# A two-expert network in a fused decoder: plain scatters into one row per choice, tables of slots with the tile innermost

## What is computed

```
x = x + L0_attn(layernorm(x)); x = x + L0_xattn(layernorm(x), ctx, mask)
x = x + L0_ffn(layernorm(x))       # below
x = x + L1_attn(layernorm(x)); x = x + L1_xattn(layernorm(x), ctx); x = x + L1_ffn(layernorm(x))

def L0_ffn(x):                     # 8 experts, 2 per token, 256 rows per expert
    top_vals, top_ids = top_k(x_flat @ router_w.T + router_b, 2)
    top_probs = softmax(top_vals)
    for e in range(8):
        tok, slot = nonzero(top_ids == e, size=256, fill_value=(N, 0))
        xin = x_pad[tok]; a = xin @ W[e]; b = xin @ V[e]
        out = out.at[tok].add((a * silu(b)) @ W_out[e] * probs_pad[tok, slot])
```

## Time and profile before

| | us |
|---|---|
| median of 3 runs (lowest, highest) | 2030.23 (2028.16, 2034.81) |
| the profiled execution | 2028.86 |
| its span in the trace | 2026.4 |
| slots stage c0, first to last vector instruction | 711.8 to 767.1 |
| two-expert stage, first gather to last vector instruction | 768.6 to 846.8 |
| wide attention, from its first ACT row | 848.6 |
| slots stage c1, first to last vector instruction | 1763.5 to 1807.7 |

### The profile page before, as it was taken

The page is one execution under the profiler, slowest core; times in us unless marked ns, Lnnn a source line. Parts: engine busy times, 40 slices in busy tenths (PEclk is TensorE's granted clock), DMA queues, the critical chain, the costliest instruction groups (busy, mean ns, idle before and its releaser), DMA issues. The chain is left out here.

```text
span 2026.4 us, 71865 instructions
## 1 busy us (share of the span) xinstructions
PE 1673.6 (83%) x28813; PEld 1383.6 (68%) x28815; DVE 1468.7 (72%) x3171; ACT 963.1 (48%) x1975; POOL 1379.7 (68%) x1173
## 2 busy tenths in 40 slices
PE   4899997899997806299899999999999659637776
PEld 3677775677776805178788888888888549536665
DVE  6888886688886691389788888888888565764443
ACT  3677775677774371033343444434343261234444
POOL 3677775677775335278788888888888427638887
PEclk9899998899998957599999999999999879869999
DMA  8100000000000322400000000000000054422221
GB/s 224 49 1 0 0 0 6 17 17 16 16 14 5 103 83 32 93 3 3 0 0 0 0 0 0 0 0 0 0 0 0 17 179 138 121 66 68 66 66 50
DMA packets 98085, 73.70 MB, mean 36 GB/s; under 512 B 11790, under 2 KB 87504, under 8 KB 97600
## 3 DMA queue, kind: packets, MB, share of 16 engines
q1 hardware_dynamic: 86176, 55.74, 9.5%
q0 software_dynamic: 8496, 15.61, 3.1%
q10 hardware_dynamic: 3312, 0.97, 0.2%
HBM read 49.19 MB, written 23.56 MB: 36 GB/s over the span
## 5 line engine op out<-in xcount | busy, mean ns | idle before, releaser
L1257 POOL TENSOR_TENSOR wa_rot<-wa_rot,wa_cross 128x1024 f32<-128x1024 f32 x128 | 302.7, 2365 | 99.6 <-DVE wa_cross L1440 99.6
L1437 DVE TENSOR_TENSOR wa_rot<-wa_ps_qk,cos 128x1024 f32<-128x1024 f32 x128 | 155.8, 1217 | 61.5 <-PE wa_ps_qk L1310 61.1
L1409 ACT COPY wa_pt<-wa_ps_svt 128x1024 f32<-128x1024 f32 x64 | 64.9, 1015 | 270.2 <-PE wa_ps_svt L1346 270.2
L333 POOL TENSOR_TENSOR sa_sd<-sa_sd,sa_mx 128x1024 f32<-128x1024 f32 x64 | 121.7, 1902 | 90.1 <-DVE sa_mx L545 90.1
L1263 POOL TENSOR_TENSOR wa_sd<-wa_sd,wa_mx 128x1024 f32<-128x1024 f32 x64 | 121.7, 1902 | 71.7 <-DVE wa_mx L1453 71.7
L333 POOL TENSOR_TENSOR ca_sd<-ca_sd,ca_mx 128x1024 f32<-128x1024 f32 x64 | 121.7, 1902 | 69.1 <-DVE ca_mx L545 69.1
L1310 PE MATMUL wa_ps_qk<-wa_xt,l_wq 128*128 128x128 f32 x1024 | 132.9, 284 | 5.8 <-issue 4.4
L1310 PE MATMUL wa_ps_qk<-wa_xt,l_wk 128*128 128x128 f32 x1024 | 134.3, 286 | 2.9 <-DVE wa_cross L1440 2.9
L1370 PE MATMUL wa_ps_o<-l_wo,wa_ot 128*128 128x128 f32 x1024 | 128.6, 280 | 8.8 <-ACT wa_ot L1415 8.8
L1310 PEld LDWEIGHTS wa_ps_qk<-wa_xt,l_wq 128*128 128x128 f32 x1024 | 120.8, 194 | 13.6 <-issue 10.7
L1370 PEld LDWEIGHTS wa_ps_o<-l_wo,wa_ot 128*128 128x128 f32 x1024 | 122.7, 196 | 9.4 <-ACT wa_ot L1415 9.4
(11 more groups left out here) (338 smaller groups left out, 4767.9 us busy)
## 6 DMA issues: line engine op xcount, KB each, us to landing
x_res<-in_x_dram SPq DMA_DIRECT2D x16, 256.0 KB, 6.7
ca_ctx_t<-in_ctx_t_dram SPq DMA_DIRECT2D x64, 64.0 KB, 1.8
x_dram<-x_res SPq DMA_DIRECT2D x16, 256.0 KB, 2.3
xn_dram<-c_xn SPq DMA_DIRECT2D x16, 256.0 KB, 2.7
x_res<-x_dram SPq DMA_DIRECT2D x16, 256.0 KB, 5.4
cs_ctx_t<-in_ctx_t_dram SPq DMA_DIRECT2D x16, 256.0 KB, 2.9
l_ffn<-in_f_w_dram SPq DMA_DIRECT2D x2, 2048.0 KB, 11.3
cm_ctx<-in_ctx_dram SPq DMA_DIRECT2D x16, 256.0 KB, 3.1
```

The lines of the kernel that those rows point to most:

```text
L333: pool.tensor_tensor(sd[:, v % 4], sd[:, v % 4], mx[:, v % 4].unsqueeze(2).to_broadcast([P, H0, SEQ]), ALU.subtract).then_inc(sub_ready, 1)
L1257: pool.tensor_tensor(rot[n][:, v % 2], rot[n][:, v % 2], cross[n][:], ALU.add)\
L1437: dve.tensor_tensor(rot[n][:, v % 2].rearrange("p f j t -> p (f j) t"), src.rearrange("p f j t -> p (f j) t"), bc(k.cos[:], 1, 2 * QUADS), ...
```

## The change

- The zeros and the store of x in xp go. A new DRAM tensor choice_dram has a row for each (choice, token). Self-attention's SP list fills it with zeros, 16 transfers of 512 KB, behind its loads; POOL clears their source first.
- The slots stage no longer lists weights (2 lists for both calls). The number of a row is choice x 8192 + token. row_hot is stored with the tile innermost [row, tile], compared in bf16 with a loaded constant `index` (2 MB, in c1 also `tile_number` of 1.2 MB; SP issues them ahead of the stores of rows). In c0 the vector engine makes all of it. Tiles go in two halves, and TensorE takes a half when it is listed; its weights are now columns 64 elements apart. In c1 the ring of normalised rows is 2 groups deep in place of 4.
- The two-expert stage scatters unweighted rows without an add and without waiting for the scatter before; ACT copies them out of PSUM. x is not loaded back: SP loads the choices' rows of 4 groups (two transfers each), and the vector engine multiplies and adds those of group 0 and takes its statistics.
- Wide attention does that for groups 1 to 15: ACT multiplies by the token's weight (`weigh`, 8 instructions), POOL adds the two choices (`pair_up`), the vector engine adds them to x (`combine`) and takes statistics. `combined_in` says in which step ACT and POOL do it. ACT waits for statistics at the start of steps 4 and 16.

```diff
+        zero_rows = None if cross else sb("zero_rows", [P, ZEROED, P])
...
+                sp.wait_ge(zeroed, 1)
+                for n in range(2 * NT // ZEROED):
+                    rows = k.choice_dram[n * ZEROED:(n + 1) * ZEROED].rearrange("n p c -> (n p) c")
+                    sp.dma_start(rows.rearrange("(q r) c -> q r c", q=P), zero_rows[:]).then_inc(zeros_stored, 16)
...
-            sp.dma_start(k.x_dram[NT:NT + NE * CAP // P].rearrange("n p c -> p n c"),
-                         bc(zero_row[:], 1, NE * CAP // P)).then_inc(zeros_stored, 16)
-            for g in range(NG):
-                sp.wait_ge(x_added, g + 1)
-                sp.dma_start(k.x_dram[rows(g)].rearrange("n p c -> p n c"), k.x_res[:, rows(g)]).then_inc(x_stored, 16)
...
+        part = sb("part", [P, 2, top, NT], BF16)
...
+        index = sb("index", [P, P, NT], BF16)
+        tile_number = sb("tile_number", [P, NT, NS], BF16) if top == 1 else None
+        row_hot = [sb(f"row_hot{n}", [P, P, NT], BF16) for n in range(top)]
...
+        by_dve = NT if top == 2 else NT * 5 // 8
+        distance = None if top == 2 else sb("distance", [P, P, NT - by_dve], BF16)
+        HALVES = [slice(0, NT // 2), slice(NT // 2, NT)]
...
+        RING = 4 if top == 2 else 2
...
+            sp.dma_start(index[:].rearrange("p a t -> p (a t)"), k.in_index.to_broadcast([P, P * NT]))\
+                .then_inc(index_loaded, 16)
...
+                for t in range(by_dve, NT):
+                    op = act.activation(distance[:, :, t - by_dve], k.iota_s[:], ACT.Square, bias=neg_part[:, t:t + 1])
+                op.then_inc(distance_ready, 1)
+                act.wait_ge(distance_ready, 1)
+                act.activation(row_hot[top - 1][:, :, by_dve:NT], distance[:], ACT.Relu, scale=-1.0, bias=one[:])\
...
+                for half in range(2):
+                    pe.wait_ge(listed_ready, 2 * n + half + 1)
+                    if HALVES[half].stop > by_dve:
+                        pe.wait_ge(hot_ready, 1)
+                    for t in range(HALVES[half].start, HALVES[half].stop):
+                        mm = pe.matmul(ps_l[:, 0:lists * NS], row_hot[n][:, :, t],
+                                       listed[n][:, t].rearrange("p l s -> p (l s)"),
+                                       start=(n == 0 and t == 0), stop=(n == top - 1 and t == NT - 1))
+            mm.then_inc(listed_made, 1)
...
+            dve.wait_ge(index_loaded, 16 if top == 2 else 32)
+            for n in range(top):
+                for half, of in enumerate(HALVES):
+                    mine = slice(of.start, min(of.stop, by_dve))
+                    op(dve.tensor_tensor(row_hot[n][:, :, mine], index[:, :, mine], bc(part[:, 1, n, mine], 1, P), ALU.is_equal))
+                    shape = [P, NT // 2, NS]
+                    op(dve.tensor_tensor(tile_hot[:, of], bc(k.iota_s[:, 0:NS], 1, NT // 2),
+                                         part[:, 0, n, of].unsqueeze(2).to_broadcast(shape), ALU.is_equal))
+                    number = (k.iota_s1[:, n * NT + of.start:n * NT + of.stop].unsqueeze(2).to_broadcast(shape) if top == 2 else
+                              tile_number[:, of])
+                    op(dve.tensor_tensor(listed[n][:, of, 0], tile_hot[:, of], number, ALU.mult))
+                    op(dve.tensor_scalar(listed[n][:, of, 1], tile_hot[:, of], k.place[:], None, ALU.mult))
+                    dve.memset(zeros[:, 0:1], 0.0).then_inc(listed_ready, 1)
...
-                op(dve.tensor_tensor(w[:, 3], w[:, 1], w[:, 2], ALU.mult))
-                op(dve.tensor_copy(parts[:, :, 0], w[:, 2:4]))
-                for n in range(3):
-                    op(dve.tensor_copy(parts_bf[:, :, n], parts[:, :, n]))
-                    if n < 2:
-                        op(dve.tensor_tensor(parts[:, :, n + 1], parts[:, :, n], parts_bf[:, :, n], ALU.subtract))
...
-                    op(dve.tensor_tensor(row_hot[n][:, 0:mine], bc(k.iota_s[:], 1, mine),
-                                         part[:, 1, n, 0:mine].unsqueeze(2).to_broadcast([P, mine, P]), ALU.is_equal))
-                op(dve.tensor_tensor(tile_hot[:], bc(k.iota_s[:, 0:NS], 1, NT),
-                                     part[:, 0, n].unsqueeze(2).to_broadcast([P, NT, NS]), ALU.is_equal))
-                op(dve.tensor_tensor(listed[n][:, :, 0], tile_hot[:], k.iota_s1[:, 0:NT].unsqueeze(2).to_broadcast([P, NT, NS]),
-                                     ALU.mult))
-                op(dve.tensor_scalar(listed[n][:, :, 1], tile_hot[:], k.place[:], None, ALU.mult))
-                for q in range(2, lists):
-                    op(dve.tensor_tensor(listed[n][:, :, q], tile_hot[:],
-                                         parts_bf[:, n, q - 2].unsqueeze(2).to_broadcast([P, NT, NS]), ALU.mult))
-                dve.memset(zeros[:, 0:1], 0.0).then_inc(listed_ready, 1)
-            dve.wait_ge(listed_made, top)
...
+                op(dve.tensor_scalar(w[:, 2], w[:, 1], 1.0, None, ALU.add))
+                op(dve.reciprocal(k.w_token[:, 0], w[:, 2]))
+                op(dve.tensor_tensor(k.w_token[:, 1], w[:, 1], k.w_token[:, 0], ALU.mult))
+            dve.wait_ge(listed_made, 1)
...
+            op(dve.scalar_tensor_tensor(out=id_i[:], in0=table[:, 0], scalar=float(P), in1=table[:, 1],
+                                        op0=ALU.mult, op1=ALU.add))
+            op(dve.tensor_scalar(k.gather_idx[:, 0:NS].bitcast(I32), id_i[:], NT * P - 1, None, ALU.bitwise_and))
+            op(dve.scalar_tensor_tensor(out=ids[:, 3], in0=table[:, 0], scalar=0.0, in1=k.empty_id[:, 0:NS],
+                                        op0=ALU.is_equal, op1=ALU.mult))
+            op(dve.tensor_tensor(k.scatter_idx[:, 0:NS], id_i[:], ids[:, 3], ALU.add))
...
+            def scatter(e):
+                pool.wait_ge(y_ready, e + 1)
+                for n in range(HALVES * e, HALVES * (e + 1)):
+                    pool.indirect_dma_start(choice_rows, bass.IndirectOffsetOnAxis(ap=k.scatter_idx[:, n:n + 1], axis=0),
+                                            y[:, n], None, bounds_check=2 * NT * P - 1, oob_is_err=False).then_inc(added[e], 16)
...
-                if e:
-                    pool.wait_ge(added[e - 1], 16 * HALVES)
-                for half in range(HALVES):
-                    n = HALVES * e + half
-                    pool.indirect_dma_start(k.x_rows, bass.IndirectOffsetOnAxis(ap=k.scatter_idx[:, n:n + 1], axis=0),
-                                            y[:, n], None, compute_op=ALU.add).then_inc(added[e], 16)
...
+                    act.copy(y[:, HALVES * e:HALVES * (e + 1)].rearrange("p n c -> p (n c)"), ps_y[:, 0:CAP])\
+                       .then_inc(y_ready, 1)
...
-            for n in range(NT // GROUP):
-                sp.dma_start(k.x_res[:, n * GROUP:(n + 1) * GROUP],
-                             k.x_dram[n * GROUP:(n + 1) * GROUP].rearrange("n p c -> p n c"))\
-                    .then_inc(k.x_loaded[n], 16)
+            for g in range(k.choice_bufs):
+                load_choices(sp, k, g)
...
-                    dve.tensor_scalar(y[:, n], ps_y[:, half * P:(half + 1) * P], k.w_slot[:, n:n + 1], None,
-                                      ALU.mult).then_inc(y_ready, 1)
...
+            def add_choices(g):
+                dve.wait_ge(k.choice_loaded[g], 32)
+                for n in range(2):
+                    if n:
+                        dve.wait_ge(added_up, 1)
+                    for m in range(GROUP):
+                        t = g * GROUP + m
+                        op = dve.scalar_tensor_tensor(out=k.x_res[:, t], in0=k.choice[:, g, n, m],
+                                                      scalar=k.w_token[:, n, t:t + 1], in1=k.x_res[:, t],
+                                                      op0=ALU.mult, op1=ALU.add)
+                    op.then_inc(added_up, 1)
+                dve.wait_ge(added_up, 2)
+            first = LoadedStats(dve, k, st, (st_ready, mv_ready, newton), 0, 1, add_choices)
...
+def load_choices(sp, k, g):
+    for n in range(2):
+        tiles = slice(n * k.tiles + g * GROUP, n * k.tiles + (g + 1) * GROUP)
+        sp.dma_start(k.choice[:, g % k.choice_bufs, n], k.choice_dram[tiles].rearrange("n p c -> p n c"))\
+          .then_inc(k.choice_loaded[g % k.choice_bufs], 16)
...
+        def combined_in(i):
+            return {0: [1], 1: [2, 3]}.get(i, [i + 2] if i + 2 < NG else [])
...
+            for g in range(k.choice_bufs, NG):
+                if g > k.choice_bufs:
+                    sp.wait_ge(combined, g - k.choice_bufs)
+                load_choices(sp, k, g)
...
+            def pair_up(g):
+                pool.wait_ge(weighed, g)
+                chosen = k.choice[:, g % k.choice_bufs]
+                pool.tensor_tensor(chosen[:, 0], chosen[:, 0], chosen[:, 1], ALU.add).then_inc(paired, 1)
...
+                    if stage is subtract_max and isinstance(i, int):
+                        for g in combined_in(i):
+                            pair_up(g)
...
```

(35 more changed lines are left out.)

186 lines of the change are left out of this document (88 added, 98 removed).

## The result

The changed kernel takes 2023.9 us (median of 15 runs, 2021.48 to 2026.35) where the kernel before takes 2030.23 (2023.22 to 2036.69): the ratio is 0.9965, with a 95% interval of 0.9953 to 0.9977. Faster by 0.35%, where 0.8% was forecast (2014). The profiled execution of the changed kernel took 2022.29 us with a span of 2020.4, against 2028.86 and 2026.4 before.

What follows compares the result with a forecast made beforehand. Stages stand in a row, each bounded by its own engines, wide attention by a vector loop as tight as TensorE's. 2028.9 - 11.6 - 22.0 + 13.2 + 6.3 - 1.0 = 2013.8, said as 2014 us; range 2001 to 2027.

Steps and rivals of the forecast that it cites:

- First slots stage: First slots stage: faster bf16 comparison in four halves, only 32 matmuls after the last list; 11.6 us saved.
- rivals 1 and 2: Slots stages: strided weights slow TensorE (2032, chance 0.10); comparison runs at one element a cycle (2022, chance 0.10).
- Two-expert stage: Two-expert stage: cheaper plain scatters and a shorter path from SP's first load to ACT's first row; 22.0 us saved.
- Wide attention: Wide attention: added vector work and a late subtraction lose 13.2 us in steps 3 to 14, 6.3 in step 2.
- Step 2: Wide attention, step 2: two additions, statistics, aggregates and scales on the vector engine; 6.3 us lost, high bound 8.
- Second slots stage: Second slots stage: ACT becomes the bound, behind the constants' loads and a ring of 2; 1.0 us saved.
- about 1778: Second slots stage: time on the old axis until which ACT, two groups sent, waits behind the constants.
- Distances 7.1 later: Second slots stage: ACT's distances end 7.1 us after its last rows at 1791.5.
- Six more groups at POOL's pace of 2.2 us: Second slots stage: ACT's six remaining groups of rows, 2.2 us each, end at 1791.5.
- Rival 5: Second slots stage: constants load at half rate, rows, distances and TensorE up to 10 us late; 2019 to 2025, chance 0.08.
- Rivals 3 and 4: Wide attention: additions hidden, steps stay 11.2 us (2001, chance 0.10); high bounds of 26 and 8 paid (2028, chance 0.08).

Runs made afterwards that it cites:

- c1_flat: Changed kernel with ACT's distances in the second slots stage written contiguously, tile outermost, and read strided by ACT's row_hot: 2019.65 us, ratio 0.9949.
- c1_act_stores: Changed kernel with ACT, not SP's queue, issuing the stores of its own rows in the second slots stage: 2014.58 us, ratio 0.9925.
- c1_no_share: Changed kernel with ACT's share of row_hot in the second slots stage given to the vector engine: 2010.08 us, ratio 0.9906.

## Why the prediction was right or wrong

*First slots stage*, 11.6 saved: 11.5. The fast comparison took 2.29 (2.3), the last list ended at 751.2 (750.9). TensorE's matmuls with strided weights took 0.094 (0.105). Right; rivals 1 and 2 fall.

*Two-expert stage*, 22.0 saved: 24.6. The scatters ran without a wait between them and the path from SP's first load to ACT's row took 11.5 (forecast 11.6), as foreseen. The issue of a plain scatter was over-priced, 1.0 where 1.14 was taken from the last stage: 16 x 0.14 makes most of the 2.6.

*Wide attention*, 13.2 and 6.3 lost: 19.6 in all, but shared otherwise. A step was 12.20 (12.3), only ten of the twelve paid in full, 9.9 in all. Step 2 lost 9.0 in this execution (7.4 to 9.0 in seven kernels with this order), above its high bound of 8:
```profile
840.33 1.65 DVE L1547 TENSOR_TENSOR x_res<-x_res,choice 128x512 f32<-128x512 f32 x1
...
850.72 3.78 PE L1361 MATMUL wa_ps_qk<-wa_xt,l_wk 128*128 128x128 f32 x16 [7.56 <-DVE wa_cross L1505]
```
Its two additions took 1.65 and 1.21 us and not 0.75, with POOL beside them, 1.4 over. And TensorE, idle for 7.56 us, came back with 3.78 us for 16 matmuls that take 2.05 in the trace before, at a granted clock of 0.50 from 850 to 855: 1.7 which no term had. The remaining 0.7 of the stage is made of 0.3 and 1.2 gained in the first and the later steps and 2.2 lost in the last ones, where 16 and 8 of TensorE's last matmuls took 3.52 and 1.91 us, against 2.05 and 1.04 before (granted clock 0.66 from 1585 to 1590, and 1.00 from 1600 to 1605 in the trace before). What the working left out is that vector engine and POOL exclude each other, and TensorE's clock after its idle time. That the sum of the stage came out at 19.6 for 19.5 is partly luck: step 2 was under-priced by 2.7, the twelve later steps over-priced by 3.3, and 0.7 fell outside both.

*Second slots stage*, 1.0 saved: 8.9 lost. This is the step that failed, and its 9.9 us are more than the whole miss (6.0 saved where the sum had 15.1). Its form was right (ACT becomes the bound, behind a ring of two and the constants; ACT's third group started at 1761.05, as "about 1778" on the old axis says), and two terms were mis-sized. "Distances 7.1 later" took the duration from the earlier trace rows although their output had become strided: 14.36. The stride was weighed for TensorE's reads and not for ACT's writes. "Six more groups at POOL's pace of 2.2 us" took POOL's pace from rows where the vector engine did other things: 18.2 us, not 13.5. So the distances started 4.6 later and lasted 7.3 longer; with 0.65 for TensorE's batch (4.0, not 3.4) that is 12.5 from the cast to the copy. c1_flat gives back the strided write, c1_act_stores 5.1 of the late start, and c1_no_share both at once. The small instructions ahead of the cast gained 2.3 which no term had: in the trace before they take 0.40 us beside POOL's rows, in the one after 0.17, with POOL waiting for the constants.

*Rival 5* gave this number, 2019 to 2025, by another cause: the constants were not slow (416 GB/s from 1750 to 1755 and 265 in the next 5 us, and ACT's third group came when forecast). *Rivals 3 and 4* fall by the step of 12.20. The context stages' 1.7 us are in no edit. TensorE's 1406 matmuls there take 117.1 us where they took 115.5, at a granted clock of 0.83 over 152 us against 0.84 over 150; why is open.
